# A three-layer graph kernel on one Trainium2 core: smaller edge groups, windows that start at any node, and gathers ahead

## The reference

```
def mlp(h, W, b, g, beta):                 # statistics over all rows of h
    h = relu(h @ W + b);  return g * (h - mean(h)) * rsqrt(var(h) + eps) + beta
node = mlp(x, Wn, ...)                      # 6250 x 96
edge = mlp(edge_attr, We, ...)              # 206250 x 96
msg  = mlp(concat(x[src], x[dst], edge), Wm, ...)
x = layernorm(x + segment_sum(msg, dst) + node)
y = x
for l in range(3):                          # 4 heads of 24 channels
    h = y @ W[l];  a_s, a_d = per-head dots of h
    e = leaky_relu(a_s[src] + a_d[dst], 0.2)
    alpha = exp(e - segment_max(e)[dst]);  alpha /= segment_sum(alpha)[dst]
    y = relu(segment_sum(h[src] * alpha) + bias[l])
return layernorm(x + y)
```

## Time and profile before

| | |
|---|---|
| median of 3 runs | 13644.67 us |
| profiled execution: span, first to last instruction | 10308.7 us |
| to the first gather of messages | 531 us |
| message stage | 2616 us |
| normalization, first table | 136 us |
| one attention layer (three of them) | 2213 us |
| between two layers | 136 us |
| after the last layer | 113 us |

### The profile page before, as it was taken

The page is one execution under the profiler, slowest core; times in us unless marked ns, Lnnn a source line. Parts: engine busy times, 40 slices in busy tenths (PEclk is TensorE's granted clock), DMA queues, the critical chain, the costliest instruction groups (busy, mean ns, idle before and its releaser), DMA issues. The chain is left out here.

```text
span 10308.7 us, 216753 instructions
## 1 busy us (share of the span) xinstructions
PE 8173.1 (79%) x57388; PEld 7347.6 (71%) x57388; DVE 5876.6 (57%) x13878; ACT 5135.3 (50%) x7222; POOL 6429.3 (62%) x6478
## 2 busy tenths in 40 slices
PE   4989999999995777777776777777777777777776
PEld 1479988999995666666666667666666666666676
DVE  7744444444445666666664666666664566666665
ACT  4522222222221666666662666666663566666663
POOL 0076666666652777777772777777771777777771
PEclk9978888888886999999996999999996999999997
DMA  3111111111111222222221222222221222222220
GB/s 93 30 40 37 36 35 35 36 35 35 35 29 21 41 41 39 39 39 39 38 39 18 41 41 40 39 39 39 38 39 17 41 41 40 39 39 39 39 39 20
DMA packets 395600, 385.81 MB, mean 37 GB/s; under 512 B 283546, under 2 KB 285082, under 8 KB 393378
## 3 DMA queue, kind: packets, MB, share of 16 engines
q0 software_dynamic: 206848, 330.54, 16.6%
q1 hardware_dynamic: 188722, 54.90, 2.9%
HBM read 362.60 MB, written 22.36 MB: 37 GB/s over the span
## 5 line engine op out<-in xcount | busy, mean ns | idle before, releaser
L670 POOL DMA_INDIRECT rows<-table_a,idx x4848 | 4722.0, 974 | 1834.7 <-issue 1463.9
L1061 DVE CUSTOM_DVE_ANT_0 work<-work,ps 128x1024 f32<-128x1024 f32 x1194 | 1458.4, 1221 | 2459.1 <-issue 1585.5
L1174 PE MATMUL ps<-rows,work 128*128 x19104 | 2470.3, 284 | 424.9 <-ACT work L1122 423.3
L1174 PEld LDWEIGHTS ps<-rows,work 128*128 128x128 f32 x19104 | 2295.6, 197 | 678.1 <-issue 668.6
L670 POOL DMA_INDIRECT rows<-table_m,idx x1616 | 1655.4, 1024 | 1389.9 <-DMA idx<-in_src_dram 907.3
L1157 PE MATMUL ps<-ident,work 128*128 128x128 f32 x9552 | 1371.4, 289 | 1189.5 <-issue 1031.0
L1157 PEld LDWEIGHTS ps<-ident,work 128*128 128x128 f32 x9552 | 1088.5, 147 | 1352.4 <-issue 1131.2
L1122 ACT ACTIVATE work<-ps 128x1024 f32<-128x1024 f32 x1194 | 1225.7, 1027 | 1146.3 <-PE ps L1157 1103.8
L1082 DVE SCALAR_TENSOR_TENSOR work<-work,rows 128x256 f32<-128x256 f32 x4776 | 1717.4, 421 | 1.3 <-DVE work L1071 0.2
L1165 PE MATMUL ps<-ident,work 128*128 128x128 f32 x9552 | 1372.0, 292 | 80.8 <-DVE work L1082 80.8
L1135 ACT ACTIVATE work<-work,small 128x1024 f32<-128x1024 f32 x1194 | 1352.7, 1133 | 0.0
(11 more groups left out here) (220 smaller groups left out, 5829.5 us busy)
## 6 DMA issues: line engine op xcount, KB each, us to landing
rows<-table_a,idx POOLq DMA_INDIRECT x4848
rows<-table_m,idx POOLq DMA_INDIRECT x1616
idx<-in_src_dram SPq DMA_DIRECT2D x808, 4.0 KB
edge_parts<-big SPq DMA_DIRECT2D x6, 1616.0 KB, 7.6
big<-edge_parts SPq DMA_DIRECT2D x202, 48.0 KB
work<-edge_parts SPq DMA_DIRECT2D x50, 192.0 KB
table_a<-work SPq DMA_DIRECT2D x3, 2474.5 KB, 23.0
big<-in_edgeT_dram SPq DMA_DIRECT2D x1, 3232.0 KB
```

Source lines behind the costliest of these rows:

```text
L670: pool.indirect_dma_start(rows[:, k, j, 0:width], None, table, bass.IndirectOffsetOnAxis(ap=idx[:, k, j:j + 1], axis=0)).then_inc(s_gat[k] ...
L1061: dve.tensor_tensor_reduce(out=logit[:, par], in0=logit[:, par], in1=ps[:, 2 * par:2 * par + 2, :].rearrange("p b n -> p (b n)"), scale=SL ...
L1174: last = pe.matmul(ps[:, 6 + par, 0:D + 1], probT[:, par, j, :], rows_of(at("slot", 3))[:, j, 0:D + 1], start=(j == 0), stop=(j == TPG - 1))
```

## The change

- Groups have 7 tiles (896 edges), 231 of them. A window is 32 nodes in both stages and starts at the lowest destination of its group (or 32 further), anywhere; one list of steps serves both kinds. Accumulators are read and written across two neighbouring rows of windows in attention (`pair_of`, `parts`), and as 32 columns of a node-wide array in the message stage.
- Message steps: the comparison comes ready turned, from a product that spreads the destinations' two digits (`pick`) and one DVE operation (`match_turned`); the three bf16 products per tile become one over a stack of the three parts; the bias and the node features go through an added row of ones and `tensor_first`.
- Attention steps: one masking operation for all heads; small operations on ACT and DVE for the two parts of a window.
- SP loads the indices of 8 groups by one DMA. POOL waits in `gather` for `freed` (slot g - 8 free) and for the steps to have come so far (`steps_told`): in messages for the edge product of step g - 1, in attention for the turned mask of step g - 2.
- The first 8 message groups (`AHEAD`) are gathered by POOL beside the edge statistics.
- Lists, message tables and node products lie in the first block beside the splitting; loads are issued from SP and ACT.
- Normalization, folding and tables are pipelined over banks of 4 tiles or chunks of 12: sums, norm, turn, product, copy and the table's DMA follow one another; the destinations' logits are four more columns of the table product. The memset of the accumulator between layers is gone.

```diff
 
-TPG = 8
+TPG = 7
 GE = P * TPG
 NG = -(-E // GE)
...
+CHUNK = 8
+NC = -(-NG // CHUNK)
+IW = CHUNK * TPG
 LAG = 4
+LEAD_M = 0
...
+            @block.gpsimd
+            def _(pool):
+                pool.wait_ge(s_tab, 16)
+                pool.wait_ge(shared["idx0"], 16)
+                pool.wait_ge(s_sent_b, 16 * 3)
+                pool.memset(acc_m[:, ESTAT:], 0.0)
+                for g in range(AHEAD):
+                    for j in range(TPG):
+                        at = g * TPG + j
+                        pool.indirect_dma_start(rows[:, g, j, 0:D], None, table_m,
+                                                bass.IndirectOffsetOnAxis(ap=idx[:, 0, at:at + 1], axis=0)).then_inc(shared[f"gat{g}"], 16)
...
-                    def gather(k, turn):
-                        pool.wait_ge(s_idx[k], turn * 16 + 16)
+                    def gather(g, k, c):
+                        if k % CHUNK == 0:
+                            pool.wait_ge(s_idx[k // CHUNK], c * 16 + 16)
+                        if not (isinstance(g, int) and g < RING):
+                            pool.wait_ge(freed, g - (RING - 1))
+                        if not (isinstance(g, int) and g < emit.paced_from):
+                            pool.wait_ge(emit.steps_told, g - emit.lead)
+                            pool.sem_inc(paced, 1)
                         pool.sem_inc(begun, 1)
                         for j in range(TPG):
-                            pool.indirect_dma_start(rows[:, k, j, 0:width], None, table,
-                                                    bass.IndirectOffsetOnAxis(ap=idx[:, k, j:j + 1], axis=0)).then_inc(s_gat[k], 16)
-                    with pool.Fori(0, NG // RING) as i:
-                        for k in range(RING):
-                            gather(k, i)
-                    for k in range(NG % RING):
-                        gather(k, NG // RING)
+                            at = k % CHUNK * TPG + j
...
-                    a = big[:, bass.ds(at("row", 2), MW)]
-                    dve.tensor_tensor(a, a, ps[:, 6 + par, 0:MW], ALU.add).then_inc(shared["done"], 1)
+                    sums = big[0:MW, bass.ds(at("node", 2), WA)]
+                    dve.tensor_tensor(sums, sums, ps[0:MW, 6 + par, 0:WA], ALU.add).then_inc(shared["done"], 1)
...
+                def match_turned(q, par, at):
+
+                    dve.wait_ge(s["dst_ready"], q + 1)
+                    if not (isinstance(q, int) and q < 2):
+                        dve.wait_ge(s["pre_ready"], 2 * q - 2)
+                    dve.tensor_scalar(eqT[:, par].rearrange("p (b n) -> p b n", b=2), ps[0:3 * WA, 0:2, 0:GE // 2],
+                                      base_w[0:3 * WA, bass.ds(at("window", 0), 1)],
+                                      selects[0:3 * WA, bass.ds(at("table", 0) + WA + 4, 1)],
+                                      ALU.subtract, ALU.is_equal).then_inc(s["eqt_ready"], 1)
+                    if not (isinstance(q, int) and q == 0):
+                        dve.wait_ge(s["win_ready"], q)
+                    dve.tensor_scalar(b_low, b_all[:, bass.ds(at("parts", 0) + ROW_B, D)],
+                                      selects[0:3 * WA, bass.ds(at("table", 0) + WA + 1, 1)], None, ALU.mult).then_inc(s["low_ready"], 1)
+                    dve.wait_ge(s["low_ready"], q + 1)
+                    dve.scalar_tensor_tensor(b_win[:, par], b_all[:, bass.ds(at("parts", 0), D)],
+                                             selects[0:3 * WA, bass.ds(at("table", 0) + WA, 1)], b_low,
+                                             ALU.mult, ALU.add).then_inc(s["win_ready"], 1)
+
...
+                    wait_positive(dve, shared["landed"], at("ready", 1), dve_wanted)
...
+                        pe.wait_ge(s["eqt_ready"], q)
+                    for at_bank, weights, told in ((0, pick[:], "dst_ready"), (2, wt["We_b"][:], "u_ready")):
+                        for half in range(2):
+                            last = pe.matmul(bank(at_bank + half, D, GE // 2), weights,
+                                             edge_ring[0:weights.shape[0], bass.ds(at("eslot", 0) + half * (GE // 2), GE // 2)],
+                                             start=True, stop=True)
+                        last.then_inc(s[told], 1)
 
                 def message_product(k, par, at):
 
-                    pe.wait_ge(s["eqts_ready"], k + 1)
+                    pe.wait_ge(s["eqt_ready"], k + 1)
...
                         pe.wait_ge(s["v_ready"], k)
-                    ut = uT[:, par].rearrange("p (e j) -> p j e", j=TPG)
-                    for j in range(TPG):
-                        o = ps[:, 4 + j // 4, (j % 4) * D:(j % 4 + 1) * D]
-                        pe.matmul(o, ut[:, j, :], W3s[:], start=True, stop=False)
-                        for v in range(3):
-                            last = pe.matmul(o, eqT[:, par, j, :], big_b[:, bass.ds(at("parts", 1) + v * D, D)],
-                                             start=False, stop=(v == 2))
-                        if j % 4 == 3:
-                            last.then_inc(s["pre_ready"], 1)
+                    ut, match = (v[:, par].rearrange("p (e j) -> p j e", j=TPG) for v in (uT, eqT))
+                    for half, (j0, j1) in enumerate(HALVES):
+                        for j in range(j0, j1):
+                            o = ps[:, 4 + half, (j - j0) * D:(j - j0 + 1) * D]
+                            pe.matmul(o, ut[:, j, :], W3s[:], start=True, stop=False)
+                            last = pe.matmul(o, match[:, j, :], b_win[:, par], start=False, stop=True)
+                        last.then_inc(s["pre_ready"], 1)
 
...
-                        last = pe.matmul(ps[:, 6 + par, 0:MW], eq[:, par, j, :], rr[:, par, j, :], start=(j == 0), stop=(j == TPG - 1))
+                        last = pe.matmul(ps[0:MW, 6 + par, 0:WA], rr[:, par, j, :], eq[:, par, j, :], start=(j == 0), stop=(j == TPG - 1))
...
+            steps_told, lead, paced_from = a_sems["t_ready"], 1, 2
...
-                    for h in range(H):
-                        source = rows_of(at("slot", 0))[:, :, D + 1 + h].unsqueeze(2).broadcast_to([P, TPG, WA])
-                        last = dve.scalar_tensor_tensor(masked[:, par, :, h, :], ne, MASKED, source, ALU.mult, ALU.add)
-                    last.then_inc(s["a_ready"], 1)
+                    dve.tensor_scalar(pen, ne, MASKED, None, ALU.mult).then_inc(s["pen_ready"], 1)
+                    dve.wait_ge(s["pen_ready"], q + 1)
+                    source = rows_of(at("slot", 0))[:, :, D + 1:D + 1 + H].unsqueeze(3).broadcast_to([P, TPG, H, WA])
+                    dve.tensor_tensor(masked[:, par], pen.unsqueeze(2).broadcast_to([P, TPG, H, WA]), source, ALU.add).then_inc(s["a_ready"], 1)
...
+                def parts(k, par, at):
+                    act.wait_ge(s["o_ready"], k + 1)
+                    for v in range(2):
+                        last = nc.scalar.activation(part_sums[:, par, v, :], ps[:, 6 + par, 0:D + 1], ACT.Copy,
+                                                    scale=selects[:, bass.ds(at("table", 3) + WA + v, 1)])
+                    last.then_inc(s["parted"], 1)
...
+        def fold(eng, c, quarters):
+            t0, t1 = span(c)
+            for h in range(H):
+                for q in quarters:
+                    of_head = slice(h * WA, (h + 1) * WA)
+                    of_window = slice(QUARTERS * t0 + q, QUARTERS * t1, QUARTERS)
+                    last = eng.tensor_tensor(folded[q * WA:(q + 1) * WA, t0:t1, h * C:(h + 1) * C],
+                                             acc[of_head, of_window, h * C:(h + 1) * C],
+                                             rden[of_head, of_window].unsqueeze(2).broadcast_to([WA, t1 - t0, C]), ALU.mult)
+            return last
```

1572 lines of the change are left out of this document (902 added, 670 removed).

## The result

The changed kernel takes 10638.82 us beside 13642.35 us for the kernel before, a ratio of 0.7794 (95% interval 0.7783 to 0.7805). I had forecast 12650 us, with a range from 11980 to 13550: the direction is right, the size is not. The profiled execution spans 10639.8 us and its time is 10641.6 us, so after the change nothing lies outside the span. That alone contradicts reading (a) of the "3336 us outside", the one that the forecast was made with: nothing fixed is added around the span here.

What follows compares the result with a forecast made beforehand. PE bounded messages and steps with register waits bounded attention, gathers close behind; POOL's gathers would bound both afterwards. Savings of 1000 us took the span from 10309 to 9310; plus 3336 outside it, 12650 us forecast, range 11980 to 13550.

Steps and rivals of the forecast that it cites:

- reading (a): The remainder is a fixed piece around the profiled span: 9310 + 3336 = 12646 us; 35%, the forecast.
- 3336 us outside: Kernel before: timed 13644.67 us against a profiled span of 10308.7; the difference appears in no profile row.
- (b): All runs are slower than the profile in proportion, 13645/10309 = 1.324, giving 12323 us; 15%.
- c: The remainder sits in the gathers, 1.93 us each before the change, giving 13430 us; 25%.
- (d): The remainder sits in the steps, 2.3 us each, still hidden under gathers, giving about 9400 us; 18%.
- Sum of 9310 us: Whole span: 10309 less 1000 saved (518 messages, 246 attention, 142, 46 and 48 between stages); bounds 9050 to 9700.
- POOL takes the place of the steps: Attention: gathers bound instead of steps, 9.13 us a group; 82 us saved a layer, 246 in all.
- Messages: POOL bounds: Message stage: gathers at 9.48 us a group lie over PE's 8.2 and DVE's 6.8; 518 us saved.
- Eight groups ahead: Edge statistics: 74 us of message gathers done early, but POOL then stands about 65, so some 10 arrive.
- The rule of the exclusive port: Edge statistics: DVE and GpSimd share an exclusive lock, so gathers there would cost more than 1.326 us each.
- Blocks between stages: Between layers 65 us for 136 (50 to 100), after messages 90 for 136, at the end 65 for 113.
- The rival of the pacing: Attention: waiting for PE's turned mask makes a 12.6 us chain, 10.8 a group; span 10450, about 13790 us; 5%.

Runs made afterwards that it cites:

- after_2: Changed kernel unaltered, run again on a chip where the kernel before needs 10269 us: 8964.4 us, ratio 0.8727.
- four_after: Changed kernel, but after each pass's first eight groups POOL gathers four of a group's seven tiles: 7753.5 us, ratio 0.5674.
- late2: Changed kernel with two small transfers between a group's landing and SP's word of it: 10615.4 us, ratio 0.7862.
- late2_free: Changed kernel with two small transfers before SP's word and POOL free to run seven groups ahead: 11539.6 us, ratio 0.8535.
- free_both: Changed kernel with both pacing waits loosened to step g - 8: 8927.6 us (0.8672); where the kernel before needs 13667 us, 11619.7 us (0.8498).
- four_before: Kernel before, but after each pass's first eight groups POOL gathers four of a group's eight tiles: 10523.3 us, ratio 0.7700.
- narrow_before: Kernel before with gathers of 24 values a row after the first eight groups: 10231.3 us (0.9955), repeated 10239.6 us (0.9976).
- after_again: Changed kernel unaltered, run again on a chip where the kernel before needs 13507 us: 10596.4 us, ratio 0.7847.
- before_w: Kernel before with a maximum with zero put ahead of its register waits: 10314.4 us, ratio 1.0003.

## Why the prediction was right or wrong, step by step

**"The 3336 us outside" (the 35, 15, 25 and 18% of a, b, c and d): wrong, and the step that failed.** The forecast of 12650 is reading (a), 9310 + 3336, with the 3336 us as a fixed piece around the span. None of the four readings holds, since the remainder does not exist on either kind: the span is 10639.8 us for a run of 10641.6 on the long kind, 8960.1 for 8961.9 on the short. It was the difference between two kinds of chip. The nearest is (d), "in the steps", and wrong in the clause that makes it a forecast: (d) has longer steps that hide under gathers. Its sum has a slip too: PE's message step, 8.2 + 2.3 = 10.5 us, would not hide under a group of 9.48. What the runs show is signals of PE that come late *because* gathers run beside the steps. In the kernel before this costs 13507 to 13667 less 10269, 3240 to 3400 us. In the changed one it costs 10596 less 8964, 1632 us. Taken as a proportion (b) gave 12323; the change also removes half of the loss, and that is what no reading had. Of the 3004 us that the result saves, some 1300 are what the change saves on the short kind (10269 less 8964), where I had forecast 1000.

**Sum of 9310 us: the mechanisms right, the size 350 us high.** After_2 spans 8960.1. The gap by terms: up to the first attention gather 103 us (2719 forecast, 2615.6 measured); from there to the last gather of all 266 (6501 and 6235); the end 23 the other way (87 forecast from the last gather, 110 measured). In the layers the term is the price of a group. I took 7 x 1.276 and 0.2 for two waits and a count, 9.13. On after_2

```profile
5005.14 0.96 POOL L790 DMA_INDIRECT rows<-table_a,idx  x1 [0.30 <-issue]
5006.40 0.94 POOL L790 DMA_INDIRECT rows<-table_a,idx  x1 [0.30 <-issue]
```

goes on for 15 gathers in a row, two group starts among them, at 1.25 us; (4645.5 - 2615.6)/231 is 8.79 a group. The waits cost nothing. The mean of 1.276 from the earlier trace rows holds longer gathers beside the usual ones: in the first layer before, 117 of 1610 take over 1.1 us, at a median of 0.947; in a layer of after_2 it is 4 of 1616. The row of one gather, 0.94 to 0.95 and 0.30 in the earlier trace rows, was the one to take. 693 groups at 0.34 less are 236 us; most of the other 30 are the two stretches between the gathers of one layer and of the next, 87 us each by my terms (22 to land and drain, 65 for the block), 74 measured.

**"POOL takes the place of the steps": right** on the short kind. After_2:

```profile
DVE work L1134 <- SPq L732: 1906.6, 693, 17.9
POOL rows L790 <- issue: 1885.7, 6087, 29.3
```

DVE waits 693 times for SP's hand-over, one wait for each group of attention and its longest in total, as forecast, and POOL is idle for its issue alone. (The "693 us or so" among the signs of being right doesn't fit my own sum, which saves 518 up to the end of the messages; they end at 2528 for 3147, 619 saved.) On the long kind the sign of being wrong is there, gathers that wait for PE's transposes. But DVE, too, stands there before a step until SP's word comes, 925 us of a layer (562 on after_2): the steps aren't behind. POOL bounds there as well, with its gathers and, at every second group, the 3.2 us in which the word from PE doesn't come: 10.7 us a group.

**One step for each group: right.** PE has 4872 transposes in L1241, 7 x 696.

**Messages: POOL bounds, but by little.** Forecast 9.48 us a group, measured (2527.9 + 1.25 - 473.9)/223 = 9.22. PE "8.2 us or less": 7.8 (four_after). The ninth gather at 474 for a forecast of 486, POOL standing 80 us for 65.

**Eight groups ahead "bring 10 us": no gain.** 8964 us with them, 8953 without in one job, 0.13% the other way, and intervals of the ratios that overlap. On the long kind these 56 gathers cut the statistics to a quarter of their pace for 65 us. Whether that costs or pays there wasn't measured.

**The rule of the exclusive port: not seen.** I had expected the gathers beside DVE's statistics to cost more than 1.326 us. The 56 of L626 take 944 ns (median) on after_2, the same as anywhere. That was the rule taken too far: the Trainium skill, SBUF — State Buffer, "Who interferes with whom", says that a DVE instruction with at most one input in SBUF, outside the two-port modes, does not contend with GpSimd. The statistics (L677) read one tile, and the 944 ns agree. On the long kind the gathers keep their pace (947 ns) and DVE, ACT and PE lose theirs.

**Blocks between stages: right.** 56 us between layers for 65 (50 to 100), 89 behind the messages for 90.

**The rival of the pacing (5%): its figures came true, its mechanism didn't.** It had a group at 10.8 us and a span of 10450; the long kind has 10.7 us and 10592, with pauses of POOL for PE's transposes. But its chain of 12.6 us isn't there: PE's transposes end before POOL's gathers do, PE's granted clock in a layer is nearly the same with pauses (0.64) and without (0.68 on after_2), 2.4 us more in the chain cost 19 us (late2), and taking the pacing away made it 924 us slower (late2_free beside late2). What comes late is the word of transposes that are done. A number that fits is no proof of its story.

Why the ratio is 0.78 on the long kind and 0.87 on the short, then, in shares of the kernel before: free_both stands at 0.867 on the short kind and 0.850 on the long one; this 0.017 I put down to fewer steps and so fewer signals, without a run of its own. The pacing brings another 0.065 (0.7847 for 0.8498, on two chips; 0.7862 for 0.8535 in one job with two trips in each), because POOL pauses after two groups and the signals catch up. That the pause is what helps is shown, and so is that late signals come through when the gathers stop: 2.1 to 2.4 us after the last one in the layers, whenever PE was done, and within 10 us in the edge statistics. That a queue lies between, and which, is argued from this and from four_before.

**What stays open.** Whether the number of gathers or their bytes do it (narrow_before fell on the short kind twice). And whether the recording has a part: the trace of after_2 holds 110244 records of completed transfers, that of after_again 29224 for the same work. The Trainium skill, NOTIFIC — the notification-queue block, "7.1 Overflow: three behaviours, one of which stalls the engine", says that the block which writes such records holds up its producers rather than lose one inside it. Engines that are held would agree with an overloaded path of this kind, and PE, whose word is the late one, has the most records of instructions (59676 of 135362). Missing records, by that page, would have to be lost elsewhere, and they alone don't make a kernel slow: four_before runs at the pace of the short kind and has 38487 such records, where the 118565 of before_w less 16 for each of the 3104 gathers left out make 68901. No run here takes the records away, so it isn't shown.

## What to carry to other kernels

Before explaining a gap between a span and a time, ask whether both are of the same chip and job: a run of the kernel before beside each experiment tells it at once. Price an operation that sets the end from the row of one undisturbed instance, not from a mean over a loop that was bound elsewhere. And a producer that runs as far ahead as its ring allows isn't free: where it can't shorten the end anyway, a wait that keeps it two groups ahead costs 0.4% on one chip and saves 8% on another.

## What the hardware showed that I had not expected

- Five chips, two kinds: the kernel before needs 10260 to 10312 us on three and 13507 to 13667 us on two, 32% more, at equal durations of the gathers (0.944 and 0.947 us), and within some per cent of DVE's and ACT's operations. PE's differ with its granted clock.
- On the long kind, where gathers follow one another every 1.25 us, the word of PE comes late to ACT, DVE and POOL (5.67 us in the row above), that of ACT and DVE to PE, ACT and DVE doesn't, and SP has the landing of a gather 0.37 us after its last packet on both kinds (after_again and after_2). Stages without gathers are the same to the instruction.
- Beside the edge statistics the gathers also hold up the register and semaphore instructions of DVE and ACT there (0.7 or 1.4 us for 0.07 at most); in the loops few are held, most of them SP's.
- With four gathers a group instead of eight nearly all of it is gone: 10523 us for 13667.
- A memset of 8 columns with a wait behind each gather takes 0.12 us and costs 0.6 to 0.7 us of distance.
